# Weight preparation of a fused scan-and-quantized-FFN layer: transposed weights gathered in SBUF and stored once per eight chunks

## The reference

```python
xn = layernorm(x)                       # x: 8 x 4096 x 1024, float32
g, v, d = xn @ Wg + bg, xn @ Wv + bv, xn @ Wd + bd
h = linear_scan(sigmoid(g) * tanh(v), a=0.001 + 0.998 * sigmoid(d))   # over the tokens
# ffn, weights ternary and activations 8 bit:
#   weight: scale = 1 / mean(|w|) over the whole matrix; wq = clip(round(w * scale), -1, 1) / scale
#   act:    scale = 127 / max(|x|) over a row;           xq = round(x * scale) / scale
y = (silu(aq(xn) @ wq(w_gate).T) * (aq(xn) @ wq(w_up).T))     # inner size 4096
out = x + h + aq(y) @ wq(w_down).T
```

## Time and profile before

| | |
|---|---|
| median of 3 runs | 7837.5 us (7835.72 to 7862.91) |
| the profiled execution | 7842.91 us, its slowest core has a span of 7841.3 us |
| spans of the eight cores | 7786.3 to 7841.3 us |
| mean granted TensorE clock, each core | 0.651 or 0.652 |
| DMA packets, core 0 | 633417, of which 492800 under 512 bytes |

### The profile page before, as it was taken

The page is one execution under the profiler, slowest core; times in us unless marked ns, Lnnn a source line. Parts: engine busy times, 40 slices in busy tenths (PEclk is TensorE's granted clock), DMA queues, the critical chain, the costliest instruction groups (busy, mean ns, idle before and its releaser), DMA issues.

```text
span 7841.3 us, 44383 instructions; the slowest of 8 cores (7786.3 to 7841.3 us)
## 1 busy us (share of the span) xinstructions
PE 1963.1 (25%) x9490; PEld 977.7 (12%) x9490; DVE 2817.1 (36%) x4453; ACT 395.7 (5%) x676; POOL 1310.5 (17%) x994
## 2 busy tenths in 40 slices
PE   0123322320000000000000044343434344435556
PEld 0122222210000000000000011121111111112222
DVE  2454445451111311113111155565656565640111
ACT  1111111110000000000000000000000000000000
POOL 0000000000100011110011034343434343430000
PEclk9966766665555555555555577676767676767778
DMA  3111111131111311113111311111111111127777
GB/s 86 57 41 43 41 46 42 42 107 41 40 39 42 107 40 41 39 42 108 42 39 42 114 29 28 34 28 34 28 33 29 33 29 33 29 91 248 238 245 237
DMA packets 633417, 529.75 MB, mean 68 GB/s; under 512 B 492800, under 2 KB 492832, under 8 KB 622912
## 3 DMA queue, kind: packets, MB, share of 16 engines
q1 hardware_dynamic: 629504, 520.49, 22.4%
q0 software_dynamic: 3648, 6.41, 0.5%
HBM read 348.25 MB, written 109.05 MB: 58 GB/s over the span
## 4 chain that ended last, share of the span: by engine, by line
DVE 29%; SPq 23%; DMA 17%; PE 10%; POOL 9%; issue 8%; ACT 2%; DVEq 1%; POOLq 0%; ACTq 0%
SPq L283 12%; PE pb L809 6%; SPq L557 4%; SPq L665 4%; DVE qci L239 3%; DVE x_grp L241 3%; POOL pqstage L269 3%; DMA wqg<-scr_wdT 3%; DVE x_grp L252 2%; DVE x_grp L250 2%; DVE qg L509 2%; POOL x_grp L244 2%; DMA pbuf<-wdown 2%; SPq L393 2%; DVE x_grp L264 2%
## 5 line engine op out<-in xcount | busy, mean ns | idle before, releaser
L689 PE MATMUL pb<-wqg,xqF_t 128*128 128x512 bf16 x2048 | 855.6, 418 | 2255.0 <-DMA xqF_t<-scr_xq 2047.4
L269 POOL TENSOR_TENSOR pqstage<-x_grp 128x512 bf16<-128x512 f32 x192 | 264.9, 1380 | 4161.5 <-DVE x_grp L266 4161.5
L693 PE MATMUL pb<-wqu,xqF_t 128*128 128x512 bf16 x2048 | 852.2, 416 | 0.0
L262 DVE TENSOR_SCALAR qt<-pbuf,wsc 128x512 f32<-128x512 f32 x192 | 94.5, 492 | 1947.5 <-DMA pbuf<-wdown 656.1
L441 PE MATMUL pb<-wqu,wqg 128*128 128x256 bf16 x3072 | 385.2, 287 | 1116.8 <-DMA wqu<-scr_xn 1116.8
L809 PE MATMUL pb<-wqg 128*128 128x512 bf16 x2048 | 483.1, 400 | 427.8 <-DMA wqg<-scr_wdT 427.6
L255 POOL TENSOR_TENSOR x_grp<-x_grp 128x512 f32<-128x512 f32 x256 | 378.1, 1477 | 1103.0 <-DVE x_grp L252 1103.0
L689 PEld LDWEIGHTS pb<-wqg,xqF_t 128*128 128x128 bf16 x2048 | 216.1, 106 | 2591.8 <-issue 2404.0
L481 PE MATMUL pb<-scal,ones_sb 128*1 128x1 f32 x6 | 0.6, 163 | 1939.5 <-DVE scal L512 1939.5
L441 PEld LDWEIGHTS pb<-wqu,wqg 128*128 128x128 bf16 x3072 | 309.8, 103 | 1169.2 <-issue 1120.2
L720 DVE SCALAR_TENSOR_TENSOR pbuf<-pb,dvecs,epi 128x512 f32<-128x512 f32 x128 | 96.1, 751 | 727.3 <-ACT epi L703 717.2
(11 more groups left out here) (89 smaller groups left out, 2565.0 us busy)
## 6 DMA issues: line engine op xcount, KB each, us to landing
wqg<-scr_wdT SPq DMA_DIRECT2D x512, 256.0 KB, 5.0
pbuf<-wdown SPq DMA_DIRECT2D x64, 512.0 KB, 4.3
pbuf<-wgate SPq DMA_DIRECT2D x64, 512.0 KB, 4.0
pbuf<-wup SPq DMA_DIRECT2D x64, 512.0 KB, 3.7
scr_pqF<-pqstage SPq DMA_DIRECT2D x32, 1024.0 KB, 3.9
wqg<-scr_pqF SPq DMA_DIRECT2D x32, 1024.0 KB, 8.2
pbuf<-x SPq DMA_DIRECT2D x32, 512.0 KB, 3.2
x_grp<-x SPq DMA_DIRECT2D x32, 512.0 KB, 4.8
```

What stands on the lines that cost most here:

```text
L269: e.tensor_tensor(o, a, b, OP.subtract), wait=(vb,))
L689: e.matmul(o, l, r, start=st, stop=sp),
L693: e.matmul(o, l, r, start=st, stop=sp),
```

## The change

The transposes of a chunk no longer go to `qtmp` or `pqroll`, but straight into `xbig`, which is the columns 8192 to 16383 of `wqu`: chunk li of a group of eight writes its block j to the columns j * 1024 + (li % 8) * 128. A chunk's eight transposes are one call with one semaphore. Nothing is stored after a chunk, but after the eighth chunk of a group, eight stores of 128 x 1024 bf16 (256 KB each, 2048 bytes per row) write the group to HBM, as soon as the transposes of the whole group have landed. The first transposes of the next group wait for these stores. The down matrix is read with the column block as the outer loop, so that a group of eight chunks is a block of whole rows of `scr_wdT`. The guard in the first tile of the next stage is taken out.

```diff
+        xbig = wqu[:, 8192:16384]
...
-        def prep_quant(load_list, sw_col, first_guard=()):
+        def prep_quant(load_list, sw_col, group_dst, first_guard=()):
...
-                xst = qtmp if li % 2 == 0 else pqroll
                 xw = [gmark]
-                if (li % 2) in xstage_st:
-                    xw.append(xstage_st[li % 2])
-                for half in range(2):
-                    emit_xpose4([qtmp4(li % 4, half * 512 + b4 * 128, 128)
-                                 for b4 in range(4)],
-                                xst[:, half * 512:(half + 1) * 512],
-                                src_wait=tuple(xw))
-                slot_xp[li % 4] = last_xpose_marks(2)
+                if li % 8 == 0 and pq_state["xbig_st"][0] is not None:
+                    xw.extend(pq_state["xbig_st"][0])
+                n = tp_state["n"]
+                tp_state["n"] += 1
+                sem = TD[n % 8]
+                if n - 8 >= 0:
+                    xw.append(tp_state["marks"][n - 8])
+                cb = (li % 8) * 128
                 for j in range(8):
-                    op("y", lambda e, i_=xst[:, j * 128:(j + 1) * 128], o=dst_fn(j):
-                       e.dma_start(out=o, in_=i_), sem=SWs[li % 4], inc=16,
-                       wait=slot_xp[li % 4] if j == 0 else ())
-                xstage_st[li % 2] = wv(SWs[li % 4])
+                    op("y", lambda e, i_=qtmp4(li % 4, j * 128, 128),
+                       o=xbig[:, j * 1024 + cb:j * 1024 + cb + 128]:
+                       e.dma_start_transpose(o, i_), sem=sem, inc=16,
+                       wait=tuple(xw) if j == 0 else ())
+                tp_state["marks"].append(wv(sem))
+                slot_xp[li % 4] = (tp_state["marks"][-1],)
+                if li % 8 == 7:
+                    gmarks = tuple(tp_state["marks"][-8:])
+                    g8 = li // 8
+                    for j in range(8):
+                        op("y", lambda e, i_=xbig[:, j * 1024:(j + 1) * 1024],
+                           o=group_dst(g8, j):
+                           e.dma_start(out=o, in_=i_), sem=SWs[j % 4], inc=16,
+                           wait=gmarks if j == 0 else ())
+                    pq_state["xbig_st"][0] = tuple(wv(s4) for s4 in SWs)
...
-                   for c in range(8) for q in range(4)]
-        prep_quant(down_l2, 4, first_guard=((SX, sx_group[NG - 1]),))
+        down_l2 = [d_wdown[c * 128:(c + 1) * 128, q * D:(q + 1) * D]
+                   for q in range(4) for c in range(8)]
+        prep_quant(down_l2, 4,
+                   lambda g8, j: scr_wdT[g8 * D + j * 128:g8 * D + (j + 1) * 128, :],
+                   first_guard=((SX, sx_group[NG - 1]),))
...
-            if ti == 0 and pc < 4 and prep_roll_guard[pc] is not None:
-                bg = bg + (prep_roll_guard[pc],)
```

More of the change, by code:

```diff
@@ L515, in qtmp4 @@
             return pqstage[:, cc * D + c0:cc * D + c0 + w]
-        pq_state = {"slot_xp": {}, "xstage_st": {}, "prev_g": [None]}
-        def prep_quant(load_list, sw_col, first_guard=()):
+        pq_state = {"slot_xp": {}, "xbig_st": [None], "prev_g": [None]}
+        def prep_quant(load_list, sw_col, group_dst, first_guard=()):
             vmarks = {}
@@ L522, in prep_quant @@
             slot_xp = pq_state["slot_xp"]
-            xstage_st = pq_state["xstage_st"]
-            for li, (src_slice, dst_fn) in enumerate(load_list):
+            for li, src_slice in enumerate(load_list):
                 buf = wchunk[li % 4]
@@ L575, in build_program @@
         prep_scalars(0, 1, 1.0 / (INNER * D))
[L576 to L580, removed]
+        prep_quant(gate_l1, 0,
+                   lambda g8, j: scr_wgT[j * 128:(j + 1) * 128,
+                                         g8 * 1024:(g8 + 1) * 1024])
         st_wg = tuple(wv(s4) for s4 in SWs)
@@ L585, in build_program @@
         prep_scalars(2, 3, 1.0 / (INNER * D))
[L586 to L590, removed]
+        prep_quant(up_l1, 2,
+                   lambda g8, j: scr_wuT[j * 128:(j + 1) * 128,
+                                         g8 * 1024:(g8 + 1) * 1024])
         st_wu = tuple(wv(s4) for s4 in SWs)
```

## The result

The changed kernel takes 7446.4 us (median of 8 runs, 7441.3 to 7460.5) against 7842.5 (8 runs): a ratio of 0.9495, 95% interval 0.9485 to 0.9506, 396 us less. The prediction said 7456, in a range of 7415 to 7530, and faster by over 0.5% at 0.93.

A forecast was written before the change was run, and what follows sets the result against it. Predicted bound: waits in `prep_quant`'s closed loop on SyncE's one in-order queue, 96 chunks of 26.2 us. Gain 411 minus 30 lost makes 381 us: 7842.9 - 381 = 7462, or 7456 on the median's footing; range 7415 to 7530.

The forecast's parts named there:

- Stores gone from 84 chunks: Chunks not ending a group lose landing wait and eight store issues before the next load: 4.89 us each, 411 us.
- The landing wait as a rival: Load behind transposes can't begin before they land, so 1.2 us return in 84 chunks: 101 us, time 7557, chance 0.12.
- The late load E: Load behind a group's 2.1 MB of stores lands E = 2.5 us later, 12 times: 30 us lost.
- the row of the 338 GB/s: Weight loads behind the up call ran at this rate; 2.1 MB then take 6.2 us, giving 2.5 us later landing.
- either bound: Limits on how much later the load behind a group's stores lands: 1.0 us from below, 4.15 from above.
- Eight large stores issue as fast as small ones: At a group's end, 256 KB stores issue like 32 KB ones; next load still 3.75 us after the first store.
- Buffer wait 0: Next group's first transposes wait for stores from the only `xbig`, but these land before SyncE gets there: 0 us.
- dearer transposes 0: Scattered destinations add nothing to 1.23 us per transpose; rival: up to 783 us more, time 8239, chance 0.04.
- Slow stores: Rival at group ends: stores stay at 71 GB/s, 2.1 MB takes 29.5 us, 309 us lost, time 7736, chance 0.04.

The follow-up runs named there:

- e2_order: Kernel before, its eight small stores of a chunk unchanged but issued behind the next chunk's load: 7402.0 us, ratio 0.9421.
- e1_land: Changed kernel with one wait more, each chunk's load waiting until the transposes of the chunk before have landed: 7546.0 us, ratio 0.9586.
- e5_again: The changed kernel itself, unaltered, measured once more: 7444.9 us, ratio 0.9496 to the kernel before.
- e4_defer: Changed kernel with a group's eight stores issued behind the next chunk's load, last group of each matrix as before: 7403.2 us, ratio 0.9415.
- e8_best: Changed kernel with next chunk's load issued ahead of the transposes, two gather buffers in turn, and a group's stores behind the next chunk's transposes: 6483.2 us, ratio 0.8265.

## Why the prediction was right

- *Stores gone from 84 chunks*, 84 x 4.89 = 411: measured 26.16 - 21.11 = 5.05 us, 84 x 5.05 = 424. From the transposes to the load it is 4.99 - 0.11 = 4.88 us (means), as forecast. Of the rest, 0.14 lies between the load and the next transposes (11.13 and 10.99): 0.02 of it is the landing, the other 0.12 VectorE's start on the landed chunk and what follows it, and its cause is not shown. Whether this was really the queue: e2_order wins 438 us by nothing but the place of the same stores.
- *The landing wait as a rival*: I gave all or nothing. e1_land shows that a fifth of it moved into the load.
- *The late load E* at 2.5 us: 23.69 - 21.11 = 2.58, close to the row of the 338 GB/s and far from either bound. That it fits so well is partly luck. The load lands 2.32 us later (5.99 against 3.67), and the other 0.22 lie between VectorE's start and the transposes (7.29 against 7.07), a step that the prediction put at nothing; these transposes carry the waits for the four semaphores of the stores, long reached, but no run takes them out alone. The sum took 3.75 us for the issues; with the measured 4.56 from the first store to the load the same row gives 6.2 - 4.56 = 1.6. And in e5_again the cost was 1.7 us on one die. It counts 9 times inside the calls, 23 us; at their three ends the stages behind lost 3.5 us together (the two mean passes 1.7, the step from the weight loads to the next transposes 1.8), less than three times 2.5. The estimate from the Trainium skill (DMA: Bandwidth & Descriptors, section "Specifications") was 2.1, inside that spread. That descriptors of one queue start in order (the Trainium skill, DMA: Bandwidth & Descriptors, section "Two DMAs through the same engine are not ordered") fits a landing of up to 6.6 us against a median of 3.6, but doesn't follow from it: in e4_defer a load that stands ahead of the stores lands 0.56 us late as well.
- *Eight large stores issue as fast as small ones*: the one term that was wrong in kind. They took 4.46 us and not 3.65, and the last chunk of a group 26.92 and not 26.16: 12 x 0.76 = 9 us. I had read it off stores of which only four stood in a row.
- *The sum*: 424 - 23 - 9 = 392, and 392.2 measured in the three calls, against 381 forecast. The gain of the first term was 13 larger than forecast and the loss of the second 7 smaller (three of the twelve late loads fall outside the calls); the third, put at nothing, took 9 of this back, so the errors cancel in part. The median moved by 396.
- *Buffer wait 0, dearer transposes 0*: no wait row for the stores; the transposes have a median of 1232 ns over 768 of them with the blocks 2 KB apart, against 1225 and 1226 before. *Slow stores*: on core 0 the 2.1 MB of a group had landed 9.1 us after the first issue (mean of 12 groups), not 29.5, so the 71 GB/s of before were no limit of the path.

What the prediction didn't see is beside its question: it called the loop closed "with nothing beside it" and asked only how much shorter it gets. Opening it by one line moved was worth 989 us in the kernel before (7840.5 to 6851.3) and 936 in the changed one, more than twice the change.

## What to carry to other kernels

When an engine's queue of DMAs is in order and a load stands in it behind work that depends on the load before, read the loop off the timeline first, and move the load ahead before making anything in the loop smaller. Larger and fewer DMAs pay by the issue time and the landing waits that they take out of a full queue (some 350 us here, once the loop was open); in a queue that waits most of the time it is enough to put them where it waits anyway. And a burst of stores has two prices, its issues and the load behind it: both are readable, as the row of the stores and the landing of the next load.

## What the runs showed of the hardware

- SyncE's time for the issue of a DMA isn't constant: the same 512 KB load takes 0.33 us with nothing in flight, 0.37 behind small stores, 0.52 right behind transposes and 0.58 behind eight stores of 256 KB. Eight stores in a row take 3.65 us at 32 KB each, 3.76 at 128 KB and 4.46 at 256 KB; the same eight of 256 KB take 5.4 us when they stand right behind a load of 512 KB (e4_defer, core 0).
- A 128 x 128 transpose from SBUF to SBUF takes the queue 1.23 us, nearly four times the 0.33 of a load of 512 KB. In e8_best this is what bounds the preparation: 96 x 10.0 of 1144 us.
